# Merging a node group on VectorE: two scale-and-add operations in place of one multiply and one add

## The chip, the core and the metric

The kernel runs on one core of a Trainium2 chip. The metric is the device time of one execution in microseconds (us), as a median over runs. The engines are TensorE (PE in the profile), VectorE (DVE), ScalarE (ACT), GpSimd (POOL) and SyncE (SP, here only a queue that issues DMAs).

## What is computed

One layer of graph attention over 12,500 nodes with 64 features and 400,000 edges that are sorted by their target node, and a residual with layer norm behind it:

```
h_src = nfeats[src]
h_dst = nfeats[dst]
z_att = concatenate([h_src, h_dst, efeats], axis=-1)
e = leaky_relu(z_att @ W_attn + b_attn, negative_slope=0.01)[:, 0]
m = concatenate([h_src, efeats], axis=-1) @ W_ne
emax = segment_max(e, dst, num_segments=N)
ex = exp(e - emax[dst])
alpha = ex / segment_sum(ex, dst)[dst]
z = segment_sum(alpha[:, None] * m, dst)
out = relu(concatenate([nfeats, z], axis=-1) @ W_out)
x = layernorm(x + out)
```

## The kernel before

**Tiles.** The edges are cut into 391 tiles of 1024 (`ST`), eight edges to each of the 128 partitions; the last one has 640. A turn is ten tiles (`RING = 10`), and there are 39 turns and the last short tile. The nodes are cut into 98 blocks of 128. A tile's targets lie in two blocks that follow each other: the mark `half[p, t, k]` is 1 for the one block of the pair (k = 0 or 1) in which partition p's node of tile t lies, and 0 for the other.

**Fetching.** POOL gathers the source nodes' rows: eight indirect DMAs for a tile (line 424), one after another, into a ring of ten slots `V`. Before a tile it waits for the tile's indices and for its slot to be free. SP brings the indices, the edge features, the targets and the scores, with a DMA each.

**A window** is the work of one tile at one pair of blocks; with these data there are 391. On VectorE it is, in program order:

- `weigh` (line 745): the exponentials' maximum, `e1`; TensorE waits for it (`mx_done`).
- lines 879 to 894: the tile's running bounds for the softmax.
- `share_out` (line 750): TensorE's sums in PSUM, `psG` (130 columns, `AW`: a count and 64 features, twice), times the two marks, into 260 columns of `psS` in PSUM. At its end it raises `merged`, for which VectorE's own next step and TensorE's next eight products into `psG` wait (line 1049).
- `merge` (line 756): the accumulator of the two blocks, 260 columns, plus these shares; raises `added`.
- `rescale` (line 761): the accumulator of the next pair times `alpha`; waits for `added`.
- from turn 7 on, in each window, a step that finishes a block: lines 788 to 792 or lines 799 and 801 by turns, and once in a turn lines 808 to 828.
- `edge_product` and `edge_score` (lines 673 and 678): the attention scores of the tile two further on. They wait for the tile's gathers (`h_in`) and its edge features. The scores go out to memory and come back spread over the partitions.

The sums in `psG` at a window belong to the window two before, so `share_out` reads blocks and marks through registers (`tb`, `bb`), that `pass_on` shifts (line 763).

ScalarE does the squared distances into `psS` (line 517), the copies of TensorE's transposes (line 500), and the exponentials (lines 535, 536). TensorE turns `e1` (line 1042) and multiplies it with the gathered rows (line 1049). The order of each engine is that of the program text; there is no scheduler. At the end VectorE merges what is still under way, raises `all_merged`, and the last blocks are finished.

Of the kernel before, what the change touches and what calls it, by code (L numbers as in the profile page):

```python
# [22 lines left out]
ALU = mybir.AluOpType  # L23
# [4 lines left out]
P = 128  # L28
# [12 lines left out]
AW = 2 * XW  # L41
# [11 lines left out]
def graph_attention(nc, x, src, dst, ef, w_ne, w_att, b_att, w_out, out):  # L53
# [19 lines left out]
    with ctx:  # L73
        def sb(name, shape, dt=F32):
            return ctx.enter_context(nc.sbuf_tensor(name, shape, dt))

        def ps(name, shape, dt=F32):
            return ctx.enter_context(nc.psum_tensor(name, shape, dt))

        def sem(name):  # L80
            return ctx.enter_context(nc.semaphore(name))
# [25 lines left out]
        accv = acc[:, :].rearrange("p (b f) -> p b f", f=AW)  # L107
# [15 lines left out]
        half = sb("half", [P, NT, 2])  # L123
# [49 lines left out]
        psS = ps("psS", [P, ST])  # L173
        psT = ps("psT", [P, 2, 512])
        psG = ps("psG", [P, 512])
# [46 lines left out]
        merged = sem("merged")  # L222
# [8 lines left out]
        added = sem("added")  # L231
        rescaled = sem("rescaled")
# [375 lines left out]
        def _(dve):  # L608
# [114 lines left out]
            g = dve.alloc_register("g_dve")  # L723
# [8 lines left out]
                dve.reg_mov(tile_of[i], 0)  # L732
                dve.reg_mov(block_of[i], 0)

            shares = psS[:, 0:2 * AW].rearrange("p (k w) -> p k w", k=2)

            def offsets():

                return (dve.snap(block_of[0], min_val=0, max_val=NB - 1), dve.snap(tile_of[2], min_val=0, max_val=NT - 1),
                        dve.snap(block_of[2], min_val=0, max_val=NB - 1), dve.snap(block_of[1], min_val=0, max_val=NB - 1))  # L740

            def weigh():

                dve.wait_ge(e_done, g)
                nc.vector.tensor_tensor(e1[:, :], zb[:, :], psE[:, :], ALU.max).then_inc(mx_done, 1)  # L745

            def share_out(tb):

                dve.wait_ge(turned, g)
                nc.vector.tensor_tensor(shares, psG[:, 0:AW].unsqueeze(1).broadcast_to((P, 2, AW)),  # L750
                                        half[:, bass.ds(tb, 1), :].rearrange("p a k -> p (a k)").unsqueeze(2).broadcast_to((P, 2, AW)), ALU.mult).then_inc(merged, 1)

            def merge(bb):

                dve.wait_ge(merged, g)
                nc.vector.tensor_tensor(accv[:, bass.ds(bb, 2), :], accv[:, bass.ds(bb, 2), :], shares, ALU.add).then_inc(added, 1)  # L756

            def rescale(bb):

                dve.wait_ge(added, g)  # L760
                nc.vector.tensor_tensor(accv[:, bass.ds(bb, 2), :], accv[:, bass.ds(bb, 2), :], alpha[:, :].unsqueeze(2).broadcast_to((P, 2, AW)), ALU.mult).then_inc(rescaled, 1)  # L761

            def pass_on():

                for i in range(LAG, 0, -1):
                    dve.reg_mov(tile_of[i], tile_of[i - 1])
                    dve.reg_mov(block_of[i], block_of[i - 1])
                dve.reg_add(block_of[0], block_of[0], 1)
                dve.reg_add(g, g, 1)
# [61 lines left out]
            def fold_group(k):  # L831

                for q in range(GROUP):
                    dve.wait_ge(rows_out[q], 16 * (k - YT + 1))
                fold(0, GROUP)

            def scale_late():

                dve.wait_ge(std_ready, late_std)
                scale(GROUP - 1, 1)  # L840
                dve.reg_add(late_std, late_std, 1)
# [21 lines left out]
            def supertile(k, s, left, y_steps=None, finishing=False):  # L863
                t = RING * k + s
                s2, k2 = (s + 2) % RING, k + (s + 2) // RING
                r = s % 2
                dve.reg_mov(block_of[0], coming_block[s])  # L867
                dve.reg_mov(tile_of[0], t)
                dve.reg_mov(scored, 16 * (RING // 2 * k + s // 2) + 16)
                with dve.Fori(0, coming_count[s]):  # L870
                    b, tb, bb, bb1 = offsets()
                    ts = bass.ds(t, 1)

                    if left == 0:
                        prepare(dve.snap(of_block, min_val=0, max_val=LAST - 1))
                        scale_late()
                    weigh()
                    dve.wait_ge(node_set, g)
                    nc.vector.tensor_tensor(picked[:, :, :], node[:, bass.ds(b, 2), :],  # L879
                                            half[:, ts, :].rearrange("p a k -> p (a k)").unsqueeze(2).broadcast_to((P, 2, 3)), ALU.mult).then_inc(wn0, 1)  # L880
                    dve.wait_ge(wn0, g)
                    nc.vector.tensor_tensor(wnode[:, :], picked[:, 0, :], picked[:, 1, :], ALU.add)

                    dve.wait_ge(lowf_in, 16)
                    dve.wait_ge(u_in[r], scored)
                    dve.wait_ge(sq_done, g)
                    nc.vector.tensor_tensor_reduce(out=um[:, :], in0=ubc[:, r, :], in1=psS[:, :], scale=1.0, scalar=-3e38,  # L887
                                                   op0=ALU.subtract, op1=ALU.max, accum_out=cmax[:, :]).then_inc(cmax_done, 1)
                    dve.wait_ge(cmax_done, g)
                    nc.vector.scalar_tensor_tensor(bounds[:, :], slopes[:, :], cmax[:, 0:1], wnode[:, :], ALU.mult, ALU.add).then_inc(bounds_done, 1)  # L890
                    dve.wait_ge(bounds_done, g)
                    nc.vector.tensor_reduce(nn[:, :], bounds[:, :], AX, ALU.min).then_inc(nn_done, 1)  # L892
                    dve.wait_ge(nn_done, g)
                    nc.vector.scalar_tensor_tensor(node[:, bass.ds(b, 2), 2], keep[:, ts, :].rearrange("p a k -> p (a k)"), nn[:, 0:1], node[:, bass.ds(b, 2), 2],  # L894
                                                   ALU.add, ALU.min).then_inc(node_set, 1)

                    share_out(tb)
                    merge(bb)
                    rescale(bb1)
                    if left == 0 or finishing and s % 2 == 1:  # L900
                        dve.reg_mov(settled, g)
                    pass_on()
                    if left == 0:
                        finish_block(dve.snap(of_block, min_val=0, max_val=LAST - 1), GROUP - 1, product)
                        dve.wait_ge(late_out, late)
                        fold(GROUP - 1, 1)
                        dve.reg_add(late, late, 16)
                        dve.reg_add(product, product, 1)
                        dve.reg_add(at_block, at_block, 1)
                        dve.reg_add(of_block, at_block, -BACK)  # L910
                        dve.reg_alu(of_block, of_block, 0, ALU.max)

                if finishing and s == 0:
                    fold_group(k)
                if finishing and s == 3:
                    dve.wait_ge(std_ready, k - YT + 1)
                    scale(0, GROUP)
                if finishing and s % 2 == 0:
                    finish_one(k, s // 2)
                if finishing and s == 0:  # L920
                    dve.wait_ge(fin_q, k - YT + 1)
                if finishing and s % 2 == 1:
                    prepare(dve.snap(finish[s // 2 + 2], min_val=0, max_val=NB - 3))
                if left >= 2:
                    done = t + 3 if isinstance(t, int) else produced
                    dve.wait_ge(ef_in[s2], 16 * k2 + 16)
                    if not isinstance(t, int):
                        dve.reg_mov(produced, t + 3)
                    dve.wait_ge(h_in[s2], 16 * J * k2 + 16 * (J if left != 2 else JL))
                    if y_steps is not None:  # L930
                        dve.wait_ge(y_ready, y_steps + 1)
                    edge_product(s2).then_inc(prod_done, 1)
                    dve.wait_ge(prod_done, done)
                    edge_score(r).then_inc(u_done, 1)
                    dve.wait_ge(u_done, done)
# [35 lines left out]
            b, tb, bb, bb1 = offsets()  # L971
            weigh()
            dve.wait_ge(alpha_done, g)
            share_out(tb)
            merge(bb)
            rescale(bb1)
            pass_on()
            b, tb, bb, bb1 = offsets()
            share_out(tb)
            merge(bb)  # L980
            dve.wait_ge(added, g)


            dve.sem_inc(all_merged, 1)
# [170 lines left out]
```

## Time and profile before

| | |
|---|---|
| median of 3 runs | 4011.47 us (4008.56 to 4011.75) |
| the profiled execution | 4011.4 us |
| its span, first to last instruction | 4009.5 us |
| granted TensorE clock, mean | 0.612 |
| VectorE busy | 3047.5 us, 76% |
| POOL busy | 2963.8 us, 74% |
| TensorE busy | 2265.5 us, 57% |
| ScalarE busy | 2138.1 us, 53% |

The profile is of one execution. Busy time leaves out register work, waits and the issuing of DMAs, so that a queue can be full at a busy share well under 100%. "issue" as what ended an idle time means that the trace shows nothing that the engine waited for.

### The profile page before, as it was taken

Reading aid. Unit: us, or ns where it says so; the run is one execution under the profiler, and the core shown is the slowest. Engines: PE = TensorE matmul, PEld = TensorE weight load, DVE = VectorE, ACT = ScalarE, POOL = GpSimd, SP = SyncE. Lnnn points to the kernel's source line nnn. Section 1 sums busy time; section 2 is a strip of 40 time slices with the busy share of each in tenths; the row PEclk is TensorE's granted clock in tenths of the full one; section 3 lists DMA queues with packets and bytes.
Section 4 is the critical chain, followed back from the end, with each engine's and each line's share of the span. In section 5 each row is a group of like instructions: output and inputs, shape, how many; then the busy total and the mean of one; then the engine's idle time right before and its main releaser. Section 6 shows DMA issues by size and latency. Waiting matters only on the chain.

```text
span 4009.5 us, 52386 instructions
## 1 busy us (share of the span) xinstructions
PE 2265.5 (57%) x10029; PEld 2009.0 (50%) x10030; DVE 3047.5 (76%) x6597; ACT 2138.1 (53%) x3582; POOL 2963.8 (74%) x3133
## 2 busy tenths in 40 slices
PE   1665665455555555555555555555555555555555
PEld 1555555455555555554555555555455554555554
DVE  8777776777777777777777777777777777777776
ACT  2665555455555555555555555555555555555554
POOL 7777777777777777777777777777777777777770
PEclk9666665656556556566665666555655666556665
DMA  7665555555555555555555555555555555555552
GB/s 164 180 173 160 158 158 158 141 154 160 158 158 159 160 160 160 158 160 157 157 159 157 159 159 160 160 160 158 159 158 157 159 159 156 159 160 160 160 159 83
DMA packets 420774, 630.65 MB, mean 157 GB/s; under 512 B 219681, under 2 KB 220065, under 8 KB 420600
## 3 DMA queue, kind: packets, MB, share of 16 engines
q1 hardware_dynamic: 307240, 521.72, 42.0%
q0 software_dynamic: 100000, 102.60, 14.6%
q10 hardware_dynamic: 13360, 4.87, 0.7%
q14 instruction: 169, 1.38, 0.1%
q8 instruction: 5, 0.08, 0.0%
HBM read 621.58 MB, written 7.07 MB: 157 GB/s over the span
## 4 chain that ended last, share of the span: by engine, by line
DVE 48%; issue 23%; POOL 13%; DVEq 8%; PE 4%; ACT 3%; DMA 0%; ACTq 0%; POOLq 0%
POOL V L424 13%; DVE um L887 10%; DVE prod L673 9%; DVE u L678 9%; DVE psS L750 4%; PE psG L1049 3%; DVE acc L756 3%; DVE acc L761 2%; DVE bounds L890 2%; DVEq L940 2%; DVE nn L892 1%; DVE picked L879 1%; DVE e L745 1%; DVEq L867 1%; ACT L568 1%
## 5 line engine op out<-in xcount | busy, mean ns | idle before, releaser
L424 POOL DMA_INDIRECT V<-in_x_dram,srcs x3125 | 2962.9, 948 | 955.1 <-issue 948.8
L1049 PE MATMUL psG<-V,pT 128*128 128x130 f32 x6250 | 1458.5, 426 | 478.4 <-DVE psS L750 478.4
L1049 PEld LDWEIGHTS psG<-V,pT 128*128 128x128 f32 x6250 | 1357.8, 329 | 612.1 <-DVE psS L750 612.1
L1042 PE MATMUL psT<-ident,e 128*128 128x128 f32 x3125 | 682.2, 387 | 1162.8 <-DVE e L745 1161.6
L1042 PEld LDWEIGHTS psT<-ident,e 128*128 128x128 f32 x3125 | 543.0, 212 | 1264.2 <-DVE e L745 1262.8
L500 ACT COPY pT<-psT 128x512 f32<-128x512 f32 x784 | 420.5, 589 | 1246.4 <-PE psT L1042 1242.8
L745 DVE TENSOR_TENSOR e<-zb,psE 128x1024 f32<-128x1024 f32 x392 | 478.7, 1221 | 381.9 <-issue 206.0
L673 DVE TENSOR_TENSOR prod<-V,psM 128x512 f32<-128x512 f32 x782 | 502.3, 684 | 90.3 <-DMA V<-in_x_dram,srcs 71.7
L887 DVE CUSTOM_DVE_ANT_0 um<-ubc,psS 128x1024 f32<-128x1024 f32 x391 | 477.5, 1221 | 96.6 <-ACT psS L517 95.7
L678 DVE TENSOR_REDUCE u<-prod 128x8 f32<-128x1024 f32 x391 | 477.0, 1220 | 13.5
L535 ACT ACTIVATE psE<-um,ebias 128x1024 f32<-128x1024 f32 x391 | 438.0, 1120 | 12.7
L517 ACT ACTIVATE psS<-dbc,nbias 128x1024 f32<-128x1024 int32 x391 | 437.8, 1120 | 12.7
L536 ACT ACTIVATE zb<-um,ebias 128x1024 f32<-128x1024 f32 x391 | 443.2, 1134 | 0.0
L756 DVE TENSOR_TENSOR acc<-acc,psS 128x260 f32 x393 | 167.3, 426 | 59.0 <-DVE psS L750 22.5
L761 DVE TENSOR_TENSOR acc<-acc,alpha 128x260 f32 x392 | 168.5, 430 | 55.9
L577 ACT COPY zTs<-psM 128x128 f32<-128x128 f32 x160 | 42.6, 266 | 257.2 <-PE psM L1076 257.2
L750 DVE TENSOR_TENSOR psS<-psG,half 128x260 f32<-128x260 f32 x393 | 171.5, 436 | 4.0 <-PE psT L1120 1.8
L512 ACT ACTIVATE nbias<-nidbias,wshift 128x1 f32 x390 | 111.8, 287 | 111.4 <-issue 100.0
L533 ACT ACTIVATE ebias<-wnode,nn 128x3 f32<-128x3 f32 x391 | 120.7, 309 | 34.3 <-DVE nn L892 33.4
L894 DVE SCALAR_TENSOR_TENSOR node<-keep,nn,node (+1 forms) x391 | 87.1, 223 | 65.1 <-DVE nn L892 63.7
L539 ACT ACTIVATE alpha<-half,ebias 128x2 f32 x391 | 109.4, 280 | 0.0
L890 DVE SCALAR_TENSOR_TENSOR bounds<-slopes,cmax,wnode 128x3 f32<-128x3 f32 x391 | 87.4, 224 | 14.0
(137 smaller groups left out, 1036.8 us busy)
## 6 DMA issues: line engine op xcount, KB each, us to landing
ubc<-scores SPq DMA_DIRECT2D x391, 512.0 KB
dbc<-in_dst_dram SPq DMA_DIRECT2D x390, 512.0 KB, 4.3
V<-in_edge_attr_dram SPq DMA_DIRECT2D x390, 256.0 KB, 3.0
V<-in_x_dram,srcs POOLq DMA_INDIRECT x3125
srcs<-in_src_dram SPq DMA_DIRECT2D x390, 4.0 KB
scores<-u SPq DMA_DIRECT2D x390, 4.0 KB
out_dram<-ro SPq DMA_DIRECT2D x159, 32.0 KB
xt<-in_x_dram ACTq DMA_DIRECT2D x6, 448.0 KB, 13.9
```

The costliest lines, as they stand in the source:

```text
L424: nc.gpsimd.indirect_dma_start(Vx[:, s, j, 1:XW], None, x[:, :], bass.IndirectOffsetOnAxis(ap=srcs[:, s, j:j + 1], axis=0)).then_inc(h_in[ ...
L500: nc.scalar.copy(pT[:, i, :], psT[:, i, :]).then_inc(pt[i], 1)
L517: nc.scalar.activation(psS[:, :], dbc[:, s % 2, :], ACT.Square, bias=nbias[:, 0:1], scale=FAR).then_inc(sq_done, 1)
L535: nc.scalar.activation(psE[:, :], um[:, :], ACT.Exp, bias=ebias[:, 1:2], scale=SLOPE)
L536: nc.scalar.activation(zb[:, :], um[:, :], ACT.Exp, bias=ebias[:, 0:1]).then_inc(e_done, 1)
L673: last = nc.vector.tensor_tensor(prod[:, k * J * F:(k + 1) * J * F].rearrange("p (j f) -> p j f", f=F), rows, wa_v[:, k:k + 1, :].broadcas ...
L678: return nc.vector.tensor_reduce(u[:, i, :], prod[:, :].rearrange("p (k j f) -> p j k f", k=2, f=F), AXY, ALU.add)
L745: nc.vector.tensor_tensor(e1[:, :], zb[:, :], psE[:, :], ALU.max).then_inc(mx_done, 1)
L750: nc.vector.tensor_tensor(shares, psG[:, 0:AW].unsqueeze(1).broadcast_to((P, 2, AW)), half[:, bass.ds(tb, 1), :].rearrange("p a k -> p (a ...
L887: nc.vector.tensor_tensor_reduce(out=um[:, :], in0=ubc[:, r, :], in1=psS[:, :], scale=1.0, scalar=-3e38, op0=ALU.subtract, op1=ALU.max, ac ...
L1042: last = nc.tensor.transpose(psT[:, i, (j - 4 * i) * P:(j - 4 * i + 1) * P], e1[:, 0:n * P].rearrange("q (p j) -> q j p", j=n)[:, j, :], i ...
L1049: last = nc.tensor.matmul(psG[:, 0:AW], pT[:, i, (j - 4 * i) * P:(j - 4 * i + 1) * P], V[:, LEADIN + s * SLOT + XW * j:LEADIN + s * SLOT + ...
```

## The change

`share_out` and `merge` become `merge_both`: two `scalar_tensor_tensor` operations, one for each block, each on 130 columns. Each reads `psG`, multiplies it by the mark as a [P, 1] operand, adds the block's accumulator and writes it back. The shares in `psS` are gone. The first operation raises `added`, the second `merged`, and `rescale` waits for both. There is no wait between the two. The operations work on other columns, so that neither reads what the other writes. At the end of the program the waits are written to match.

```
-            shares = psS[:, 0:2 * AW].rearrange("p (k w) -> p k w", k=2)
...
-            def share_out(tb):
+            def merge(tb, bb, k):
+
+                b = bass.ds(bb + k, 1)
+                return nc.vector.scalar_tensor_tensor(accv[:, b, :].rearrange("p b f -> p (b f)"), psG[:, 0:AW], half[:, bass.ds(tb, 1), k],
+                                                      accv[:, b, :].rearrange("p b f -> p (b f)"), ALU.mult, ALU.add)
+
+            def merge_both(tb, bb):
 
                 dve.wait_ge(turned, g)
-                nc.vector.tensor_tensor(shares, psG[:, 0:AW].unsqueeze(1).broadcast_to((P, 2, AW)),
-                                        half[:, bass.ds(tb, 1), :].rearrange("p a k -> p (a k)").unsqueeze(2).broadcast_to((P, 2, AW)), ALU.mult).then_inc(merged, 1)
-
-            def merge(bb):
-
+                merge(tb, bb, 0).then_inc(added, 1)
+                merge(tb, bb, 1).then_inc(merged, 1)
+
+            def rescale(bb):
+
+                dve.wait_ge(added, g)
                 dve.wait_ge(merged, g)
-                nc.vector.tensor_tensor(accv[:, bass.ds(bb, 2), :], accv[:, bass.ds(bb, 2), :], shares, ALU.add).then_inc(added, 1)
-
-            def rescale(bb):
-
-                dve.wait_ge(added, g)
                 nc.vector.tensor_tensor(accv[:, bass.ds(bb, 2), :], accv[:, bass.ds(bb, 2), :], alpha[:, :].unsqueeze(2).broadcast_to((P, 2, AW)), ALU.mult).then_inc(rescaled, 1)
...
-                    share_out(tb)
-                    merge(bb)
+                    merge_both(tb, bb)
                     rescale(bb1)
...
             dve.wait_ge(alpha_done, g)
-            share_out(tb)
-            merge(bb)
+            merge_both(tb, bb)
             rescale(bb1)
+            dve.wait_ge(rescaled, g)
             pass_on()
             b, tb, bb, bb1 = offsets()
-            share_out(tb)
-            merge(bb)
+            merge_both(tb, bb)
             dve.wait_ge(added, g)
+            dve.wait_ge(merged, g)
```

On VectorE's queue a window's merge looks like this before, from the end of the bounds on (ISA and REGISTER_ALU rows are register work that the queue does itself):

```order
L894 SCALAR_TENSOR_TENSOR node<-keep,nn,node 128x2
L750 ISA
L750 TENSOR_TENSOR psS<-psG,half 128x260
L756 ISA
L756 TENSOR_TENSOR acc<-acc,psS 128x260
L761 ISA
L761 TENSOR_TENSOR acc<-acc,alpha 128x260
L766 ISA
```

And with the change:

```order
L895 SCALAR_TENSOR_TENSOR node<-keep,nn,node 128x2
L749 ISA
L749 SCALAR_TENSOR_TENSOR acc<-psG,half,acc 128x130
L749 ISA
L749 REGISTER_ALU
L749 SCALAR_TENSOR_TENSOR acc<-psG,half,acc 128x130
L762 ISA
L762 TENSOR_TENSOR acc<-acc,alpha 128x260
L767 ISA
```

The number of operations is the same, and each of the two has half the columns; between them stand two rows of register work for the second block's address where one stood. The whole queue grows from 1020 to 1053 rows as listed. TensorE's queue is the same.

## Rows read from the trace of the kernel before

**Rows 1.** The profile's page: busy time of each engine, then the chain's shares by engine.

```profile
PE 2265.5 (57%) x10029; PEld 2009.0 (50%) x10030; DVE 3047.5 (76%) x6597; ACT 2138.1 (53%) x3582; POOL 2963.8 (74%) x3133
...
DVE 48%; issue 23%; POOL 13%; DVEq 8%; PE 4%; ACT 3%; DMA 0%; ACTq 0%; POOLq 0%
```

**Rows 2.** POOL's instructions in order: start us, us, what, [idle before it <- releaser].

```profile
4.59 1.11 POOL L424 DMA_INDIRECT V<-in_x_dram,srcs  x1 [2.88 <-DMA srcs<-in_src_dram]
...
3912.48 0.94 POOL L424 DMA_INDIRECT V<-in_x_dram,srcs  x1 [0.30 <-issue]
...
3918.72 0.94 POOL L424 DMA_INDIRECT V<-in_x_dram,srcs  x1 [0.30 <-issue]
```

**Rows 3.** POOL's waits, whole span: us in total, times, longest us.

```profile
POOL V L424 <- issue: 948.8, 3113, 0.3
```

**Rows 4.** VectorE's waits from 60 to 750 us, same columns.

```profile
DVE prod L673 <- DMA V<-in_x_dram,srcs: 71.7, 44, 3.0
...
DVE e L745 <- issue: 22.0, 8, 4.3
```

**Rows 5.** VectorE's waits from 750 us to the end.

```profile
DVE e L745 <- issue: 184.0, 31, 6.3
...
DVE um L887 <- ACT psS L517: 82.2, 32, 2.7
```

**Rows 6.** POOL in order: last gathers of tiles 71, 80 and 380.

```profile
726.60 0.94 POOL L424 DMA_INDIRECT V<-in_x_dram,srcs  x1 [0.30 <-issue]
...
817.08 0.94 POOL L424 DMA_INDIRECT V<-in_x_dram,srcs  x1 [0.30 <-issue]
...
3822.58 0.94 POOL L424 DMA_INDIRECT V<-in_x_dram,srcs  x1 [0.30 <-issue]
```

**Rows 7.** VectorE in order: products of tiles 71, 80, 380, 389 and 390.

```profile
730.55 1.28 DVE L673 TENSOR_TENSOR prod<-V,psM 128x512 f32<-128x512 f32 x2 [2.07 <-DMA V<-in_x_dram,srcs]
...
830.55 1.28 DVE L673 TENSOR_TENSOR prod<-V,psM 128x512 f32<-128x512 f32 x2
...
3863.01 1.29 DVE L673 TENSOR_TENSOR prod<-V,psM 128x512 f32<-128x512 f32 x2
...
3951.09 1.28 DVE L673 TENSOR_TENSOR prod<-V,psM 128x512 f32<-128x512 f32 x2
...
3960.31 1.28 DVE L673 TENSOR_TENSOR prod<-V,psM 128x512 f32<-128x512 f32 x2
```

**Rows 8.** VectorE's groups by line: count, busy us, mean ns, idle before them.

```profile
L750 DVE TENSOR_TENSOR psS<-psG,half 128x260 f32<-128x260 f32 x393 | 171.5, 436 | 4.0 <-PE psT L1120 1.8 <-PE psT L1042 1.6 <-issue 0.3
L761 DVE TENSOR_TENSOR acc<-acc,alpha 128x260 f32 x392 | 168.5, 430 | 55.9
L756 DVE TENSOR_TENSOR acc<-acc,psS 128x260 f32 x393 | 167.3, 426 | 59.0 <-DVE psS L750 22.5
L890 DVE SCALAR_TENSOR_TENSOR bounds<-slopes,cmax,wnode 128x3 f32<-128x3 f32 x391 | 87.4, 224 | 14.0
...
L801 DVE SCALAR_TENSOR_TENSOR fout<-zs,xt 128x64 f32<-128x64 f32 x161 | 36.3, 226 | 23.2
...
L810 DVE SCALAR_TENSOR_TENSOR ro<-fm,fout 128x320 f32<-128x320 f32 (+1 forms) x34 | 16.5, 484 | 1.2
```

**Rows 9.** VectorE in order around one merge, from 2004 us.

```profile
2004.68 0.22 DVE L894 SCALAR_TENSOR_TENSOR node<-keep,nn,node  x1 [0.17 <-DVE nn L892]
2004.83 0.44 DVE L750 TENSOR_TENSOR psS<-psG,half 128x260 f32<-128x260 f32 x1
2005.42 0.43 DVE L756 TENSOR_TENSOR acc<-acc,psS 128x260 f32 x1
2005.98 0.43 DVE L761 TENSOR_TENSOR acc<-acc,alpha 128x260 f32 x1
```

**Rows 10.** The chain that ended last, from 3955 us: start us, us, what.

```profile
3966.80 0.45 DVE psS L750
...
3967.37 3.80 PE psG L1049 x16
```

More of the change, by code:

```diff
@@ L745, in weigh @@
                 nc.vector.tensor_tensor(e1[:, :], zb[:, :], psE[:, :], ALU.max).then_inc(mx_done, 1)
-            def share_out(tb):
-                dve.wait_ge(turned, g)
-                nc.vector.tensor_tensor(shares, psG[:, 0:AW].unsqueeze(1).broadcast_to((P, 2, AW)),
-                                        half[:, bass.ds(tb, 1), :].rearrange("p a k -> p (a k)").unsqueeze(2).broadcast_to((P, 2, AW)), ALU.mult).then_inc(merged, 1)
-            def merge(bb):
-                dve.wait_ge(merged, g)
-                nc.vector.tensor_tensor(accv[:, bass.ds(bb, 2), :], accv[:, bass.ds(bb, 2), :], shares, ALU.add).then_inc(added, 1)
+            def merge(tb, bb, k):
[3 more added lines that the diff above has]
+            def merge_both(tb, bb):
+                dve.wait_ge(turned, g)
+                merge(tb, bb, 0).then_inc(added, 1)
+                merge(tb, bb, 1).then_inc(merged, 1)
             def rescale(bb):
                 dve.wait_ge(added, g)
+                dve.wait_ge(merged, g)
                 nc.vector.tensor_tensor(accv[:, bass.ds(bb, 2), :], accv[:, bass.ds(bb, 2), :], alpha[:, :].unsqueeze(2).broadcast_to((P, 2, AW)), ALU.mult).then_inc(rescaled, 1)
@@ L973, in _ @@
             dve.wait_ge(alpha_done, g)
-            share_out(tb)
-            merge(bb)
+            merge_both(tb, bb)
             rescale(bb1)
+            dve.wait_ge(rescaled, g)
             pass_on()
             b, tb, bb, bb1 = offsets()
-            share_out(tb)
-            merge(bb)
+            merge_both(tb, bb)
             dve.wait_ge(added, g)
+            dve.wait_ge(merged, g)
             dve.sem_inc(all_merged, 1)
```

## The prediction

> **What bounds the kernel now.** The page comes first: no engine is busy for more than 76% of the span, VectorE and POOL being near each other at the top, and VectorE holds 48% of the chain that ended last, with 23% "issue" beside it [rows 1]. That names a candidate and no proof, since both engines have work that the busy time leaves out. So the second view is POOL's list in order of time. The first gather starts at 4.59 us and the last of 3125 at 3918.72 [rows 2], which is 3914.13 / 3124 = 1.253 us each, and the waits say that POOL waited for nothing but its own issuing, 3113 times for 0.3 us [rows 3]. POOL is a second full queue: it runs from start to end at its own pace and finishes at 3919.66, and no change on VectorE can make it end sooner.
>
> The third view is how far VectorE is behind it. The product of a tile (line 673) can start when the tile's eighth gather has landed. Until 750 us VectorE waits there 44 times [rows 4]: tile 71's last gather ends at 727.54 (726.60 + 0.94) and the product starts at 730.55, and over the waiting tiles that distance is 2.3 to 3.4 us, which I take as landing time, 2.8. From 750 us on, in the turns that also finish blocks, there is no such wait among VectorE's waits [rows 5]. Tile 80: 818.02 and 830.55, a lag of 12.5. Tile 380: 3823.52 and 3863.01, a lag of 39.5 [rows 6, 7]. The 30 turns between them took VectorE (3863.01 - 830.55) / 30 = 101.08 us each and POOL (3822.58 - 817.08) / 30 = 100.18. VectorE is the slower by 0.90 us a turn, 0.09 us a window, and pays that as a growing lag. The last product starts at 3960.31 [rows 7], 40.7 us behind the last gather, and what follows it takes 4009.5 - 3960.3 = 49.2 us. So what VectorE can save before the tail is what it is behind, no more, however much shorter a window becomes.
>
> **The change, part by part.**
>
> The merge before: the multiply starts at 2004.83, the add at 2005.42, the rescale at 2005.98, 1.15 us from the first to the third [rows 9]. Each has 260 columns and takes 426 to 436 ns [rows 8], and 0.14 to 0.15 passes from an end to a start that waits for it.
>
> The merge after: one operation on 130 columns. From L801 (64 columns, 226 ns) to L756 (260 columns, 426 ns) a column costs 200 / 196 = 1.02 ns [rows 8], so 130 columns with a constant as scalar make 226 + 66 x 1.02 = 293 ns. The mark is a [P, 1] operand. L890 has such an operand and takes 224 ns for 3 columns, where the same line would give 226 - 61 x 1.02 = 164; that is 60 ns more. I take 293 + 60 = 353 ns for each. The second does not wait for the first. The nearest rows for two operations with register work between them and nothing to wait for are L894 and L750: L894 starts at 2004.68, lasts 0.22 and L750 starts at 2004.83, before its end by 0.07 [rows 9]. So the second starts 0.28 after the first and ends at 0.63, and the rescale starts at 0.63 + 0.15 = 0.78. Saved: 1.15 - 0.78 = **0.37 us a window**, 3.7 a turn. Bounds: without the 60 ns, 0.22 + 0.29 + 0.15 = 0.66, a saving of 0.49; with no overlap and a gap of 0.15 between the two, 0.35 + 0.15 + 0.35 + 0.15 = 1.00, a saving of 0.15. No row shows such an operation with its first source in PSUM. The nearest are L756, which reads PSUM, and L761, which does not: 426 and 430 ns [rows 8], so I add nothing. The Trainium skill, "VectorE: DVE Perf Modes", section on the TRN2 errata, gives a fixed 120 cycles from PSUM against 58 from SBUF; by it each operation would cost some 65 ns more and the saving would be an estimated 0.24. The two rows do not show that difference, and the total below would be the same.
>
> The turn with this saving takes VectorE 101.08 - 3.7 = 97.4 us, POOL still 100.2. Whatever lag the first finishing turns build then falls by 2.8 us a turn, and VectorE waits for gathers again, as it did until 750 us. At tile 71 the lag was 3 us, at tile 390 it is 40.7: 38 us over 319 windows, so that any saving over **0.12 us a window** gives the same end. At a turn's end VectorE stands still for 184.0 / 31 = 5.9 us, and it waits 82.2 / 32 = 2.6 for ScalarE soon after [rows 5], so it will be behind by a few us there and catch up by 9.98 - 8.65 = 1.3 us a window. In the last turn that is done before tile 389. Its last gather ends at 3912.48 + 0.94 = 3913.42 [rows 2] and its product starts at 3916.2. Tile 390 has five gathers only, so VectorE's own pace decides: 3960.31 - 3951.09 = 9.22 [rows 7], less 0.37, is 8.85, and its product starts at 3925.1. **First term: 3960.3 - 3925.1 = 35.2 us earlier.**
>
> The tail has four merges. TensorE's products into `psG` wait for `merged`, which comes at 0.63 instead of 0.44. In the steady windows nobody notices the 0.19. In the tail it lies on the chain: the multiply at 3966.80 releases 3.80 us of products, which then decide [rows 10], and the same shape stands at the next two windows. That costs 3 x 0.19 = 0.57. The fourth merge ends all at once at 0.63, where multiply and add took 0.59 + 0.43 = 1.02: 0.39 back. **Second term: +0.2 us.** The wait for `rescaled` that is added near the end lies beside TensorE's last products, worth 0. If these ran under it, it would cost the 0.15 of a waited start.
>
> Hidden at no price: `psS` is no longer overwritten by VectorE, but ScalarE writes it later, behind its own waits. SP's queue is driven by VectorE's scores and only gets earlier work. POOL was never held by a slot or an index, with VectorE close behind it until 750 us and far behind it later, so it stays as it is [rows 3].
>
> Sum: -35.2 + 0.2 = -35.0 on the profiled execution's 4011.4, which is 3976.4. The median of the runs is 4011.47, 0.07 from it, so the same number holds for the median.
>
> **The rivals.**
>
> Half rate. An operation with two tensor sources and a multiply and an add might take two cycles a column. Then each costs 353 + 130 x 1.02 = 486 ns, the second starts at 0.41, the rescale at 1.05, and 0.10 us a window is saved. The lag then falls by 0.1 us a turn only, and 0.10 over the 319 windows from tile 71 on is 32 us; `merged` is late by 0.46, three times, less 0.1 at the end. Time 4011.4 - 32 + 1.3 = 3980.7. Against it stands L810: 320 columns with both tensors in SBUF at 484 ns [rows 8], a full column in 1.02 ns and no more. The Trainium skill, "Vector Engine (DVE) Microarchitecture Reference", section "Points that are easy to get wrong", says that such an operation with two non-bf16 SBUF sources runs at half throughput. L810 disagrees, and here only one source is in SBUF. Chance 0.05.
>
> The turn's end grows. The idle time at a turn's end was 22.0 / 8 = 2.75 us in the short loop body and 5.9 in the long one [rows 4, 5], so it may grow with the length of the queue, and the change adds two rows of register work a window. Another such step of 3.2 us a turn leaves 0.5 us a turn saved, 0.05 a window: 0.05 x 319 = 16 us, 3995. Chance 0.04.
>
> The other side: the second operation is held. If it starts only when the first has ended and its two rows of register work are done after that, and the rate is half too, the pair takes 0.49 + 0.15 + 0.49 + 0.15 = 1.28 us, 0.13 more than now. A turn becomes 102.4 us, the lag grows by 2.2 a turn, and the last product starts 0.13 x 319 = 42 us later; `merged` comes 0.69 later, three times 0.7. Time 4011.4 + 42 + 2 = 4055. It decides from a pair over 1.15 us on. For it speaks that no row has this form; against it, [rows 8, 9] as above. Chance 0.03.
>
> No gain. A pair of 1.13 to 1.15 us, from one of these causes in part, or another limit at the present pace that VectorE only seems to set, as the 23% of "issue" in the chain [rows 1] would allow: 4005 to 4011. Chance 0.03.
>
> **How the numbers follow.** The forecast, a pair anywhere under 1.03 us, holds 0.85. Its own range is small: landing at 2.3 or 3.4 instead of 2.8 moves it by -0.5 or +0.6, the tail's terms by 1, and POOL's pace by some 2, since the three runs of before spread over 3.2 us. That is 3972.5 to 3980. The range goes on to 3984 to take in half rate with a little more in the tail. About 0.2% (8 us) is what a measurement of this kernel can tell from no change. Faster by more than that: forecast, half rate, the turn's end, 0.94. Within it: 0.03. Slower: 0.03.
>
> **What would show each step.** Right: the two operations at 350 ns or so each, 0.28 us apart, and the rescale 0.78 after the first; waits of `prod` for gathers in all turns, some hundreds in place of 44; POOL unchanged, ending at 3919 to 3921; the product of tile 390 about 5.5 us behind the last gather instead of 40.7. Wrong: a pair over 1.03 us; VectorE's idle time at a turn's end well over 6 us; POOL ending later or waiting for slots; or waits of VectorE for ScalarE at line 888 that take up what was saved.

## The result, and the profile after

The changed kernel takes 3984.45 us as a median of four runs (3981.66 to 3986.47), beside 4011.57 before. The ratio is 0.9934, with a 95% interval of 0.9916 to 0.9951: 27 us faster, where 35 were forecast, and 0.45 us above the upper end of the range.

The page's L424 and L673 groups (columns: busy us, mean ns, idle before, releaser), and its chain by engine, which [rows 1] showed with 48% VectorE:

```profile
POOL 74%; issue 24%; POOLq 1%; DVE 1%; PE 0%; DMA 0%; ACT 0%; DVEq 0%; ACTq 0%
...
L424 POOL DMA_INDIRECT V<-in_x_dram,srcs x3125 | 2971.2, 951 | 954.9 <-issue 952.2
...
L673 DVE TENSOR_TENSOR prod<-V,psM 128x512 f32<-128x512 f32 x782 | 502.5, 684 | 116.5 <-DMA V<-in_x_dram,srcs 99.3
...
L749 DVE SCALAR_TENSOR_TENSOR acc<-psG,half,acc 128x130 f32 x786 | 241.7, 348 | 4.4 <-PE psT L1120 2.3
L762 DVE TENSOR_TENSOR acc<-acc,alpha 128x260 f32 x392 | 170.2, 434 | 85.8 <-DVE acc L749 85.8
```

The chain has gone over to POOL, as forecast. But POOL's own gathers, whose mean I took as given, went from 948 to 951 ns, 8.3 us over 3125 of them. One window in VectorE's order, the answer to [rows 9]:

```profile
2006.24 0.22 DVE L895 SCALAR_TENSOR_TENSOR node<-keep,nn,node  x1 [0.18 <-DVE nn L893]
2006.43 0.61 DVE L749 SCALAR_TENSOR_TENSOR acc<-psG,half,acc 128x130 f32 x2
2007.27 0.43 DVE L762 TENSOR_TENSOR acc<-acc,alpha 128x260 f32 x1 [0.22 <-DVE acc L749]
```

The operation costs 348 ns, the pair ends 0.61 after its start, and the rescale starts 0.84 after it, 0.22 and not 0.15 behind the pair. VectorE's waits from 750 us to the end, the answer to [rows 5]:

```profile
DVE e L744 <- issue: 182.4, 31, 6.4
...
DVE um L888 <- ACT psS L517: 103.9, 66, 3.2
...
DVE prod L673 <- DMA V<-in_x_dram,srcs: 24.6, 35, 1.9
DVE um L888 <- issue: 11.3, 30, 0.7
```

The idle time at a turn's end is as before (5.9 us); the wait for ScalarE's squares has grown from 82.2 to 103.9 us, and once in a turn 0.38 us pass ahead of `um` with nothing that VectorE waited for, which the kernel before does not have. VectorE waits for gathers again, but only 35 times in these 31 turns, with 24.6 us. The end, POOL and then VectorE, where [rows 2] and [rows 7] had 3918.72, 3951.09 and 3960.31:

```profile
3919.38 0.94 POOL L424 DMA_INDIRECT V<-in_x_dram,srcs  x1 [0.30 <-issue]
3920.63 0.94 POOL L424 DMA_INDIRECT V<-in_x_dram,srcs  x1 [0.30 <-issue]
...
3926.87 0.94 POOL L424 DMA_INDIRECT V<-in_x_dram,srcs  x1 [0.30 <-issue]
```

```profile
3925.75 1.29 DVE L673 TENSOR_TENSOR prod<-V,psM 128x512 f32<-128x512 f32 x2 [1.91 <-DMA V<-in_x_dram,srcs]
...
3934.34 1.29 DVE L673 TENSOR_TENSOR prod<-V,psM 128x512 f32<-128x512 f32 x2
```

So against the sum: POOL ends at 3927.8 instead of 3919.7, 8.1 us late; the last product is 6.5 us behind it and not 5.4; and the tail takes 3984.4 - 3934.3 = 50.1 us instead of 49.4. That is 9.9 us on the span of this execution, the slowest of the four.

**Where POOL's 8.1 us are.** In POOL's list most gathers take 940 to 950 ns and some far more. Counting those over 0.97 us ("stretched" from here on) and what they take beyond 0.944, the kernel before has 93 with 14.3 us in all, the changed one 130 with 22.3. The other gathers (943.5 and 943.7 ns on average) and the gaps (952.2 us in both) are the same. One such case:

```profile
1798.41 0.43 DVE L762 TENSOR_TENSOR acc<-acc,alpha 128x260 f32 x1 [0.22 <-DVE acc L749]
1798.46 1.20 POOL L424 DMA_INDIRECT V<-in_x_dram,srcs  x1 [0.30 <-issue]
```

The rescale was under way when the gather started, and the gather took 0.26 longer. I asked this of every operation of VectorE: was it in flight at a gather's start, with over 0.15 us to run, and was that gather then longer by over 0.03? For the rescale: 63 of 64 times before, 97 of 116 after. For lines 812 and 828 (811, 813 and 829 after) most times. In the steady windows hardly for anything else, in hundreds of cases (`e1` 0 of 325, the product 0 of 346, the new merge 0 of 133). What these few lines share is that both tensors they read lie in SBUF. All others of any length read one of the two from PSUM or have one tensor only. That became theory A. It leaves out one thing: the operations of 2 to 6 columns (lines 880, 891 and 895) read two tensors from SBUF too, and stretched no gather (0 of 43 in the changed kernel), so it takes columns as well.

The rescales after which the gather was not longer are of one kind: all but one or two of them had started only 0 to 0.04 us ahead of it, and there the rescale itself took 0.46 to 0.50 us instead of 0.43. Where the gather was longer, it was so by what was left of the rescale less 0.13 us.

### The profile page after: what moved, and what is told of

It is laid out like the page before. It is cut to its first block, busy times and chain, and to the rows that moved or that the text cites. A ratio compares the mean times of both kernels' runs of the same rounds, so it can differ in the third digit from the quotient of the medians.

```text
span 3984.4 us, 53171 instructions
## 1 busy us (share of the span) xinstructions
PE 2231.2 (56%) x10029; PEld 1987.7 (50%) x10030; DVE 2970.1 (75%) x6597; ACT 2137.9 (54%) x3582; POOL 2972.1 (75%) x3133
## 4 chain that ended last, share of the span: by engine, by line
POOL 74%; issue 24%; POOLq 1%; DVE 1%; PE 0%; DMA 0%; ACT 0%; DVEq 0%; ACTq 0%
POOL V L424 74%; POOLq L442 0%; PE psG L1049 0%; POOLq L433 0%; DMA V<-in_x_dram,srcs 0%; DVE um L888 0%; DMA srcs<-in_src_dram 0%; PE psE L1128 0%; DVE prod L673 0%; DVE u L678 0%; DVE acc L749 0%; PE psT L1124 0%; DVE e L744 0%; POOLq L73 0%; PE psT L1042 0%
## 5 line engine op out<-in xcount | busy, mean ns | idle before, releaser
L424 POOL DMA_INDIRECT V<-in_x_dram,srcs x3125 | 2971.2, 951 | 954.9 <-issue 952.2
L1042 PE MATMUL psT<-ident,e 128*128 128x128 f32 x3125 | 648.6, 373 | 1016.9 <-DVE e L744 1014.8
L1042 PEld LDWEIGHTS psT<-ident,e 128*128 128x128 f32 x3125 | 519.0, 209 | 1119.2 <-DVE e L744 1116.9
L673 DVE TENSOR_TENSOR prod<-V,psM 128x512 f32<-128x512 f32 x782 | 502.5, 684 | 116.5 <-DMA V<-in_x_dram,srcs 99.3
L678 DVE TENSOR_REDUCE u<-prod 128x8 f32<-128x1024 f32 x391 | 477.1, 1220 | 13.5
L749 DVE SCALAR_TENSOR_TENSOR acc<-psG,half,acc 128x130 f32 x786 | 241.7, 348 | 4.4 <-PE psT L1120 2.3
L1072 PEld LDWEIGHTS psM<-wz,zTs 128*128 128x128 f32 x322 | 75.6, 288 | 10.0 <-issue 8.7
## 6 DMA issues: line engine op xcount, KB each, us to landing
xt<-in_x_dram ACTq DMA_DIRECT2D x6, 448.0 KB, 13.5
```

The source lines that it names most:

```text
L424: nc.gpsimd.indirect_dma_start(Vx[:, s, j, 1:XW], None, x[:, :], bass.IndirectOffsetOnAxis(ap=srcs[:, s, j:j + 1], axis=0)).then_inc(h_in[ ...
L673: last = nc.vector.tensor_tensor(prod[:, k * J * F:(k + 1) * J * F].rearrange("p (j f) -> p j f", f=F), rows, wa_v[:, k:k + 1, :].broadcas ...
L678: return nc.vector.tensor_reduce(u[:, i, :], prod[:, :].rearrange("p (k j f) -> p j k f", k=2, f=F), AXY, ALU.add)
L749: return nc.vector.scalar_tensor_tensor(accv[:, b, :].rearrange("p b f -> p (b f)"), psG[:, 0:AW], half[:, bass.ds(tb, 1), k], accv[:, b, ...
L1042: last = nc.tensor.transpose(psT[:, i, (j - 4 * i) * P:(j - 4 * i + 1) * P], e1[:, 0:n * P].rearrange("q (p j) -> q j p", j=n)[:, j, :], i ...
```

## The experiments

**The rescale's second source in PSUM, and its twin.** The edit to the changed kernel, and the twin's in the last line:

```
-  nc.vector.tensor_tensor(accv[:, bass.ds(bb, 2), :], accv[:, bass.ds(bb, 2), :], alpha[...], ALU.mult)
+  nc.vector.scalar_tensor_tensor(accv[:, bass.ds(bb, 2), :], psS[:, 0:2 * AW]..., 0.0, accv[:, bass.ds(bb, 2), :], ALU.mult, ALU.add)
...
+  nc.vector.scalar_tensor_tensor(accv[:, bass.ds(bb, 2), :], keep[:, 0:AW, :]..., 0.0, accv[:, bass.ds(bb, 2), :], ALU.mult, ALU.add)
```

> The changed kernel, with the rescale's second source in PSUM: acc times alpha is left out, and in its place stands acc plus 0.0 times 260 columns of psS, an operation of the same size at the same place. Theory A (a gather that starts while an operation of VectorE with two tensors in SBUF is under way is held until that ends; the rescale is the main such operation): the stretched gathers (over 0.97 us) fall from 130 to 30 to 50 and their extra time from 22 to under 8 us, POOL ends near 3915 instead of 3928.8, and the time is 3984 - 14 = 3970. Theory B (the new merge operations, or the DMAs' own traffic, stretch the gathers): 130 stretched gathers as now, 3982 to 3986.

> The twin of the run with psS: the same form of operation in the rescale's place, alpha left out again, but with the 0.0 times a constant table in SBUF, so both tensors are in SBUF. Theory A: 110 to 150 stretched gathers, 18 to 26 us of extra time, 3981 to 3987. If leaving alpha out or the form of the operation were what frees POOL, this one would be at 3970 too.

Measured: 3977.11 us with psS (ratio 0.9911, 0.9895 to 0.9928) and 3991.59 with the SBUF table (0.9949, 0.9932 to 0.9965), side by side on one chip: 14.5 us between the medians of two kernels that differ in where one operand lies. By the count, 38 stretched gathers with 7.9 us against 120 with 22.0, 14.1 us apart. The page's group, with psS and then with the table:

```profile
L424 POOL DMA_INDIRECT V<-in_x_dram,srcs x3125 | 2956.7, 946 | 955.0 <-issue 952.2
```

```profile
L424 POOL DMA_INDIRECT V<-in_x_dram,srcs x3125 | 2976.8, 953 | 955.2 <-issue 952.4
```

In the psS run 79 of the rescales had over 0.15 us to run at a gather's start and none stretched it; with the table 79 of 94 did. Neither leaving alpha out nor the form of the operation frees POOL; the place of the operand does. Both medians are above their forecasts (3970, and 3981 to 3987). In the profiled executions the two are 19.1 us apart: 14.1 of stretched gathers and 6 of plain ones, of which more stands under the hardware below. The psS run's profiled execution took 3971.43 us and its other three 3977 to 3980.

**More of the same cause.** The edge product's weights from SBUF:

```
-  wa_v[:, k:k + 1, :].broadcast_to((P, J, F)), ALU.mult)
+  wa[:, 2 * k * F:(2 * k + 1) * F].unsqueeze(1).broadcast_to((P, J, F)), ALU.mult)
```

> The changed kernel, with the edge product's weights read from their copy in SBUF instead of PSUM: same result, 782 operations of 684 ns now have both tensors in SBUF. Theory A: nearly every window holds a gather's start inside 1.28 us of such work, for 0.3 us on average or more, so several hundred stretched gathers, over 100 us of extra time, POOL ends after 4030 and the time is over 4070. Theory B: no more stretched gathers than now, 3982 to 3988.

Measured: 4058.08 us, one run. 394 stretched gathers, 95.6 us:

```profile
L424 POOL DMA_INDIRECT V<-in_x_dram,srcs x3125 | 3044.6, 974 | 954.8 <-issue 952.1
...
L673 DVE TENSOR_TENSOR prod<-V,wa 128x512 f32<-128x512 f32 x782 | 507.2, 690 | 192.7 <-DMA V<-in_x_dram,srcs 178.4
```

The direction and the count are theory A's, the size is under its "over 100 us": the products held gathers for 69.6 us, 0.18 us a window and not 0.3. Between the pair of products a gather is let in (of those that started 0.55 to 0.63 us behind the first product's start none was stretched). POOL ended at 4001 us in this run, 73 later than in the changed kernel, and the time rose by about as much.

**The changed kernel once more.**

> The changed kernel as it is, beside the others of this call on the same chip, to learn how far its own executions differ. Expected 3982 to 3990. If POOL sets the end, what differs between two executions is POOL's end, by the count of stretched gathers and by the length of the plain ones (943 or 948 ns), not VectorE's work.

Measured: 3984.99 us (3984.34 to 3986.83; ratio 0.9940, 0.9923 to 0.9957), 132 stretched gathers with 22.8 us, POOL's end at 3928.4. The plain gathers were alike here (943.7 ns). The count is no accident of one execution.

**The overlap undone.**

```
                 merge(tb, bb, 0).then_inc(added, 1)
+                dve.wait_ge(added, g)
                 merge(tb, bb, 1).then_inc(merged, 1)
```

> The changed kernel, with a wait of the second merge operation for the first: the overlap is undone. The pair should take 0.35 + 0.15 + 0.35 and the rescale start 1.02 us after the first (0.84 now). My account (VectorE has more to give than it needs; POOL sets the end): the window is longer by 0.2 us, the lag of the last product is longer by 0 to 6 us, time 3984 to 3991. If VectorE still set the pace, 391 x 0.18 = 70 us would come on top, and all of the gain would be gone.

Measured: 4080.61 us (ratio 1.0167, 1.0150 to 1.0184): slower than before by 67 us, and this expectation fell in two ways. One window:

```profile
2002.15 0.35 DVE L749 SCALAR_TENSOR_TENSOR acc<-psG,half,acc 128x130 f32 x1
2002.76 0.35 DVE L749 SCALAR_TENSOR_TENSOR acc<-psG,half,acc 128x130 f32 x1 [0.26 <-DVE acc L749]
2003.33 0.43 DVE L763 TENSOR_TENSOR acc<-acc,alpha 128x260 f32 x1 [0.22 <-DVE acc L749]
```

The wait costs 0.26 because the two rows of register work come behind it, and the rescale starts 1.18 after the first operation, not 1.02, which is more than the 1.15 of before. So all that the change takes out of the window is the missing wait. But 0.03 x 319 is 10 us and not 67. The rest had to come from something that I had priced at nothing, and I took it to be this: `merged` is raised at 0.96 instead of 0.44. That was theory C. The steps of VectorE from tile 80 to 380 show that it can be a part only. The turn takes 103.10 us, 2.02 more than before: 0.31 from the first merge operation to the rescale, 0.39 because that operation starts 0.19 and not 0.15 us behind the start of the bounds' last one, 0.67 of waits of `um` for ScalarE, 0.39 ahead of `um` with nothing waited for, and some 0.25 in small steps. The second and the fourth are in the changed kernel too.

**The release alone, late.** The kernel before, with TensorE released by the add:

```
-  share_out:  nc.vector.tensor_tensor(shares, ...).then_inc(merged, 1)
-  merge:      dve.wait_ge(merged, g); nc.vector.tensor_tensor(accv..., shares, ALU.add).then_inc(added, 1)
+  share_out:  nc.vector.tensor_tensor(shares, ...).then_inc(added, 1)
+  merge:      dve.wait_ge(added, g); nc.vector.tensor_tensor(accv..., shares, ALU.add).then_inc(merged, 1)
```

(In short form; the rescale and the end of the program wait for `merged` accordingly.)

> The kernel before, with TensorE's release moved from the end of the multiply to the end of the add, 0.58 us later, and nothing else: VectorE has the same operations and waits. Theory C (a late release reaches VectorE: products, then the z transpose, ScalarE's copy of it, ScalarE's squares, for which VectorE's um waits): VectorE's wait for ScalarE grows from 96 us to about 180 or more, and the time from 4012 to 4070 to 4120. Rival, my prediction's step (TensorE has room, nobody notices outside the tail): 4012 plus 3 x 0.6 = 4014.

Measured: 4037.55 us against 4009.43 (ratio 1.0071, 1.0054 to 1.0088): 28 us, so the steady windows do notice, though less than theory C asked. VectorE's waits in it:

```profile
DVE um L887 <- ACT psS L517: 159.6, 98, 3.3
```

The chain can be read from the third window of a turn of this run (columns as in [rows 9]):

```profile
2084.31 3.84 PE L1049 MATMUL psG<-V,pT 128*128 128x130 f32 x16 [1.30 <-DVE acc L756]
...
2088.26 0.42 PE L1076 MATMUL psM<-ident,zs 128*128 128x128 f32 x1
2088.72 0.27 ACT L577 COPY zTs<-psM 128x128 f32<-128x128 f32 x1 [1.99 <-PE psM L1076]
...
2089.00 1.28 ACT L567 ACT_TABLE_LOAD   x1
...
2090.62 1.28 ACT L568 ACT_TABLE_LOAD   x1
...
2092.34 1.12 ACT L517 ACTIVATE psS<-dbc,nbias 128x1024 f32<-128x1024 int32 x1
...
2093.62 1.22 DVE L887 CUSTOM_DVE_ANT_0 um<-ubc,psS 128x1024 f32<-128x1024 f32 x1 [3.24 <-ACT psS L517]
```

The products start when VectorE releases them, the z transpose stands behind them on TensorE, ScalarE's copy waits for it, the squares stand behind the copy, and `um` needs the squares. In this window, once in a turn, ScalarE also loads two tables of 1.28 us each between the copy and the squares, which is most of the wait. From tile 80 to 380 the wait of `um` is 2.58 us a turn before and 3.34 here, nearly all in the third window of a turn (2.58 and 3.11), and the turn grows from 101.08 to 101.81. In the first 70 tiles, where the copies of the y step stand in that place, the waits add up to 13.4 and 51.7 us, which cost nothing there: the product of tile 71 starts at 728.8 us, and before at 730.6. The changed kernel waits 3.25 a turn, and 31.4.

**One merge operation less.** Left out is the sum for the second block:

```
-                merge(tb, bb, 0).then_inc(added, 1)
-                merge(tb, bb, 1).then_inc(merged, 1)
+                merge(tb, bb, 0).then_inc(merged, 1)
```

The waits for `added` go with it.

> The changed kernel without its second merge operation: the second block's sums are left out, the rescale starts 0.3 us sooner and TensorE is released at 0.35 instead of 0.61. If POOL sets the end, these 0.3 x 391 = 110 us bring almost nothing: the last product a few us behind the last gather as now, 3978 to 3986. If VectorE still set it in part, 3950 or less. By theory C VectorE's wait for ScalarE falls from 135 us to under 96.

Measured: 3974.49 us (ratio 0.9916, 0.9899 to 0.9932). VectorE waits 237.0 us for gathers instead of 106.0, so it has that much more to give, and the time moves by 10.5 only. All of that is POOL: it ends at 3918.1 instead of 3928.4, with 93 stretched gathers and 12.4 us instead of 132 and 22.8. The span ends 54.1 us behind POOL here and 55.1 there. The part on theory C was wrong in number: the wait for ScalarE is 131.2 us, not under 96, and 130.2 in the changed kernel beside it. TensorE is released sooner here than in the kernel before (0.35 and not 0.44), and `um` still waits as long as in the changed kernel. So the longer waits of `um` in the changed kernel are not put down to the late release by any run. That an earlier `um` waits for the same squares whatever TensorE does fits them, and is argued.

**The rescale on ScalarE, in both kernels.** Besides the operations, the step at lines 788 to 792 goes behind the edge product, since it now waits for ScalarE, and ScalarE keeps the block's number itself. The added ScalarE lines (without the wait for `merged` in the kernel before) stand between its two exponentials, and VectorE's added wait ahead of the merge:

```
+  act.wait_ge(added, g); act.wait_ge(merged, g)
+  for k in range(2):
+      last = nc.scalar.activation(accv[:, last_block + k, :], accv[:, last_block + k, :], ACT.Identity, scale=alpha[:, k:k + 1])
+  last.then_inc(rescaled, 1)
...
-                    rescale(bb1)
+                    dve.wait_ge(alpha_done, g)
```

> The changed kernel with the rescale on ScalarE, as two operations of 130 columns between the two exponentials, and the step that reads its result moved behind the edge product: same result. By theory A the stretched gathers fall to 30 to 50 and POOL ends 14 us sooner, for 3970, if VectorE, 0.6 us shorter in each window, still keeps up. Against it: ScalarE gets 0.6 us more a window and VectorE waits for its squares already; if that wait grows by over 0.6 us a window, VectorE sets the pace again and the time is over 4000.

> The kernel before, multiply and add as they were, with only the rescale moved to ScalarE and the step that reads its result moved behind the edge product: same result. VectorE saves the rescale, about 0.57 us a window, more than the 0.12 it needs to keep up with POOL, and few gathers are stretched: 3968 to 3978, as fast as the changed kernel with the same move. If what the changed kernel gains came from the two merge operations as such, this one would be 8 us or more slower than that.

> The changed kernel with the rescale on ScalarE once more, on the same chip as the run beside it: 3969 to 3975, POOL's end near 3913, 30 to 50 stretched gathers.

Measured: 3971.49 us for the changed kernel with this move (ratio 0.9905, 0.9888 to 0.9921), and in a second measurement 3979.12 (0.9911, 0.9895 to 0.9928) beside 3977.81 for the kernel before with the same move (0.9905, 0.9889 to 0.9922), on a chip where the kernel before took 4015.52. The page's groups of the first:

```profile
L424 POOL DMA_INDIRECT V<-in_x_dram,srcs x3125 | 2955.7, 946 | 954.8 <-issue 952.4
...
L686 DVE TENSOR_TENSOR prod<-V,psM 128x512 f32<-128x512 f32 x782 | 502.0, 683 | 230.7 <-DMA V<-in_x_dram,srcs 202.1
```

Stretched gathers: 30, with 6.7 us. ScalarE did become tighter (`um` waits for it 281.4 us), but VectorE still waits 202.1 us for gathers. And with VectorE's rescale out of the way it makes no difference which merge the kernel has (1.3 us between the two): both end at POOL's pace, at 3919.0 and 3919.8 us, and what is left to win is POOL's. The three measurements with the move have ratios of 0.9905, 0.9911 and 0.9905 to the kernel before, the changed kernel 0.9934 and 0.9940. Side by side on one chip stand 0.9905 and 0.9940, 13.5 us apart; the other intervals touch or overlap.

## Why the prediction was right or wrong

- **What bounds the kernel.** Right. POOL sets the end, the chain says so, VectorE falls back to it, and a VectorE lighter by another 0.3 us a window (the run with one merge) gained nothing beyond what POOL gave.
- **"POOL was never held by a slot or an index [...] so it stays as it is."** This step failed: POOL's pace was priced at no change, and it ended 8.1 us later, of the 9.9 by which the profiled execution missed the forecast (the median missed it by 8.05, and that has no profile of its own). The step looked only at what POOL waits for ahead of a gather. The trace's waits can't show a gather that takes longer once started, and the 948 ns of the page was already a mean over 944 ns and 93 long ones. The Trainium skill, "SBUF — State Buffer", section "SBUF: two separate sides", has the rule that I should have weighed: VectorE and GpSimd share one pair of SBUF ports, and a VectorE operation with two SBUF inputs can hold it against GpSimd's reads. The runs agree (14.5 us between the psS run and its twin). The change removed no such operation and added none; it moved when the rescale comes.
- **Why more gathers were caught after.** This stays open. Of the 220 windows from tile 160 to 380, the rescale stretched a gather in 35 before, 56 and 57 in two executions after, and 33 with one merge. It does so if it starts some 0.04 to 0.28 us ahead of the gather, a fifth of the 1.25 us from gather to gather, so that windows without any pattern would give some 42 (an estimate from these figures). Before, a turn of VectorE took 0.9 us longer than one of POOL, so that each rescale drifted past the gathers; after, both have the same turn and the same windows are hit again: the eighth of a turn in 12 of 22 turns, in both executions. But the locking by itself does not raise the count: the kernel with the late release drifts by 1.06 us a turn and stretched 55 in the same windows, and the one with one merge is locked and stretched 33. Where in POOL's 1.25 us the rescales come to lie decides, and that the change moved them to a worse place is bad luck as far as these runs go. No run shifted only the phase.
- **The pair.** 348 ns against 353, and 0.61 against 0.63: right. The rescale starts at 0.84 and not 0.78, since 0.22 and not 0.15 passes behind the pair. Saved are 0.31 us and not 0.37, and 0.04 of that goes again because the first operation starts 0.19 and not 0.15 behind line 895. The bound "no overlap and a gap of 0.15 [...] 1.00" was no bound: the run with the wait took 1.18.
- **"The turn with this saving takes VectorE [...] 97.4 us."** Wrong in size. From tile 80 to 380 a turn took 100.16 us with 0.70 of waits for gathers in it, so VectorE's own share is 99.46: 1.6 us saved a turn and not 3.7. The merge gives some 2.7, and 1.05 of that goes into the longer idle time ahead of `um` (0.67 for ScalarE, 0.38 with nothing shown). POOL's turn was 100.18, so VectorE had 0.7 us a turn to spare and not 2.8, and the forecast's "some hundreds" of waits for gathers are 77 and 88 in the two executions. The conclusion that VectorE falls back to POOL held, by a thinner margin than the working says.
- **"In the steady windows nobody notices the 0.19."** Wrong as a rule, shown by the late release (28 us for 0.58). What it costs in the changed kernel no run shows by itself; whatever it is was hidden, because VectorE has room.
- **The last product.** It was 6.5 us behind POOL and not 5.4: the product of tile 389 started 4.2 us after its gather's end and not 2.8, and that of tile 390 came 8.60 after it and not 8.85.
- **The tail.** +0.9 instead of +0.2 us (the second execution had 49.5 us, +0.3). Counted from the last product, the three groups of TensorE's products on the chain start 0.16, 0.65 and 1.14 us later than before, where the forecast had 0.19 for each, and the last merge gives 0.33 back. What lies in the two steps of 0.49 I did not follow further.
- **The rivals.** Half rate: L749 at 348 ns excludes it. (The 484 ns of L810 in [rows 8] are a mean over two forms; its 320 columns take 492, which says the same.) The turn's end: 5.9 us as before, with the 0.38 us a turn ahead of `um` as the only new idle time of this kind. The held second operation did come true, but in the kernel with the wait, at 1.18 us and 4081.

## What to carry to other kernels

When an engine leaves the chain, the engine that takes it over is no constant: look at what the first one does to it, not only at what it waits for. In these runs an operation of 64 columns or more that reads two tensors from SBUF on VectorE held up most gathers that started under it, by up to the rest of its own length; reading one of the two from PSUM, or doing the operation on ScalarE, took that away. And a semaphore that releases another engine has a place of its own in the sum, in every window: follow it until it comes back.

## What the runs showed of the hardware

- A gather is lengthened only if VectorE's operation is in flight when it starts. A gather that is under way when the rescale starts is not: the rescale ran fully inside gathers in the other windows, at 430 ns and with no stretch. If the rescale starts up to 0.04 us ahead of the gather, or up to 0.02 behind its start, it is the rescale that takes longer (0.44 to 0.50 us).
- The single-source operation at line 792 (793 in the changed kernel; 128 columns, SBUF to SBUF) stretches a gather seldom and by little. In the changed kernel it did so in 0 of 40 cases, in the psS run in 5 of 29, by 28 to 48 ns, each time having started 0.11 to 0.14 us ahead of the gather. (Two other single-source operations, at lines 696 and 699, held one gather each for 0.15 us in the kernel before, at 53 and 54 us.) It was itself stretched: it takes 0.29 us as a rule, but one that starts 0.46 to 0.7 us into a gather ends 0.99 us after that gather's start, whenever it started, and so takes up to 0.53.
- The plain gathers have one of two lengths for a whole execution, whatever the kernel: on average 943.5 to 943.8 ns or 945.6 to 945.8. The psS run's profile has the first and its twin's the second, on one chip, which is 6 us over 3125 gathers. A kernel that POOL bounds carries that difference in full. It is most of what put the twin's 3991 and the second ScalarE run's 3979 above their forecasts, and a reason to compare such kernels by medians taken side by side.
